# GpSimd instead of VectorE copies the low parts of the expert weights, in halves, four slots ahead

## The reference, cut to what matters

```
router_logits = xf @ router_w.T                 # 8192 tokens, 8 experts
topv, topi = top_k(softmax(router_logits), 2)   # two experts for each token
g = xf @ gate_w[e] + gate_b[e]                  # 128 -> 256
u = xf @ up_w[e] + up_b[e]                      # 128 -> 256
h = silu(g) * u
expert_out = h @ down_w[e] + down_b[e]          # 256 -> 128
y = sum over the token's two experts of probs * expert_out
```

## Time and profile before

| what | us |
|---|---|
| median of 3 executions without profiler | 1462.38 (1460.31 to 1465.81) |
| span of the profiled execution, first to last instruction | 1622.8 |
| what lies around the span | the profile gives no time of the profiled execution but its span |
| first expert stage in the profile (first row load to last scatter) | about 777 to 1041 |
| second expert stage in the profile | about 1314 to 1574 |

### The profile page before, as it was taken

The page is one execution under the profiler, slowest core; times in us unless marked ns, Lnnn a source line. Parts: engine busy times, 40 slices in busy tenths (PEclk is TensorE's granted clock), DMA queues, the critical chain, the costliest instruction groups (busy, mean ns, idle before and its releaser), DMA issues. The chain is left out here.

```text
span 1622.8 us, 37888 instructions
## 1 busy us (share of the span) xinstructions
PE 1206.8 (74%) x11717; PEld 1014.2 (62%) x11717; DVE 1149.5 (71%) x3828; ACT 943.0 (58%) x2002; POOL 980.7 (60%) x1152
## 2 busy tenths in 40 slices
PE   3779998888888888972688788476766357887850
PEld 1557777776777777752688787355555257877850
DVE  5379998888888888864555555388888645555538
ACT  2478888887888888841444444266666334444420
POOL 4245687777777777676255555438788735555540
PEclk9599999999999999996789898799899679998875
DMA  7121111111111111131222222112222132222228
GB/s 206 53 76 47 43 58 55 56 56 57 57 57 57 56 57 57 36 116 52 77 75 77 80 77 71 59 51 71 77 80 67 41 90 77 76 77 74 77 72 283
DMA packets 100819, 120.94 MB, mean 75 GB/s; under 512 B 17945, under 2 KB 80721, under 8 KB 100369
## 3 DMA queue, kind: packets, MB, share of 16 engines
q1 hardware_dynamic: 69600, 75.85, 15.9%
q0 software_dynamic: 17280, 35.95, 6.5%
q10 hardware_dynamic: 13744, 6.75, 1.5%
HBM read 49.45 MB, written 44.46 MB: 58 GB/s over the span
## 5 line engine op out<-in xcount | busy, mean ns | idle before, releaser
L1096 DVE TENSOR_TENSOR ebuf<-score_banks,region 128x768 f32<-128x768 f32 x256 | 243.8, 952 | 40.4 <-PE score_banks L809 34.8
L1337 ACT ACTIVATE region<-ebuf 128x768 f32<-128x768 f32 x256 | 215.4, 858 | 21.8 <-DVE ebuf L1096 21.8
L1315 ACT CAST copied<-max_banks 128x768 bf16<-128x768 f32 x256 | 205.4, 802 | 29.6 <-PE max_banks L797 27.3
L1755 POOL DMA_INDIRECT choice_rows<-first_yo,first_xg x142 | 136.7, 963 | 134.4 <-DVE first_yo L1875 100.0
L1755 POOL DMA_INDIRECT choice_rows<-second_yo,second_xg x142 | 137.3, 967 | 126.8 <-DVE second_yo L1875 92.4
L1625 POOL DMA_INDIRECT expert_rows<-d_rows,a_d_index x128 | 131.7, 1029 | 42.5 <-issue 30.8
L2171 POOL DMA_INDIRECT expert_rows<-d_rows,z_d_index x128 | 131.6, 1028 | 38.4 <-issue 32.1
L1831 ACT ACTIVATE first_silu<-first_bgu,first_biases 128x256 f32<-128x256 f32 x142 | 63.2, 478 | 131.6 <-PE first_bgu L1784 63.0
L1831 ACT ACTIVATE second_silu<-second_bgu,second_biases 128x256 f32<-128x256 f32 x142 | 63.1, 477 | 126.2 <-issue 61.3
L1514 POOL TENSOR_TENSOR rs<-arg,neghalf 128x4 f32<-128x4 f32 x32 | 37.1, 1161 | 137.8 <-DVE arg L1028 137.8
L1867 DVE SCALAR_TENSOR_TENSOR second_hT<-second_bgu,second_biases,second_silu 128x256 f32<-128x256 f32 x142 | 64.1, 478 | 74.9 <-ACT second_silu L1831 45.1
(11 more groups left out here) (333 smaller groups left out, 4386.0 us busy)
## 6 DMA issues: line engine op xcount, KB each, us to landing
region_r<-region_r SPq DMA_DIRECT2D x192, 128.0 KB
first_xg<-expert_rows SPq DMA_DIRECT2D x71, 132.0 KB
second_xg<-expert_rows SPq DMA_DIRECT2D x71, 132.0 KB
z_rows<-choice_rows SPq DMA_DIRECT2D x32, 256.0 KB
c_rows<-choice_rows SPq DMA_DIRECT2D x16, 512.0 KB
out<-xres ACTq DMA_DIRECT2D x16, 256.0 KB
choice_rows<-first_yo,first_xg POOLq DMA_INDIRECT x142
choice_rows<-second_yo,second_xg POOLq DMA_INDIRECT x142
```

Source lines behind the costliest of these rows:

```text
L1096: nc.vector.tensor_tensor(ebuf[:, half_of_ebuf(c, j), :, :], score_banks[:, :, 0:BK], bias32[:, plain(j), :], ALU.add).then_inc(scores_fre ...
L1315: nc.scalar.copy(copied[:, 2 * j:2 * j + 2, :], max_banks[:, :, 0:BK]).then_inc(maxed_free, 1)
L1337: nc.scalar.activation(p32[:, j % 4, :, :], ebuf[:, half_of_ebuf(c, j), :, :], ACT.Exp).then_inc(exped, 1)
L1755: pool.indirect_dma_start(choice_dram, bass.IndirectOffsetOnAxis(ap=xg[:, i % G, t, E:E + 1].bitcast(I32), axis=0), yo[:, i % 4, t, :], No ...
```

## The change

`wlo` gets four buffers in place of two. DVE no longer copies it. POOL copies it in two halves of 128x256 (gate, up). The halves of slot i + 4 stand behind the two scatters of slot i, one behind each; those of slots 0 to 3 stand ahead of the first scatter. POOL loads the packed word of experts for itself, once in four slots, and waits for `gu_full` of slot i before it overwrites that slot's buffer. PE waits for two increments of `wl_ready` for each slot in place of one. Nothing that is computed changes.

```diff
-        whi, wlo = sb("whi", [P, 2, 2 * EF], F32R), sb("wlo", [P, 2, 2 * EF], F32R)
+        whi, wlo = sb("whi", [P, 2, 2 * EF], F32R), sb("wlo", [P, 4, 2 * EF], F32R)
...
             @block.gpsimd
             def _(pool):
-
+                def lower_weights(i, e, parts):
+
+                    if i >= 4:
+                        pool.wait_ge(gu_full, i * NF + (NF - 4 * NF))
+                    for k in parts:
+                        at = slice(k * EF, (k + 1) * EF)
+                        nc.gpsimd.tensor_copy(wlo[:, i % 4, at], w["lo"][:, bass.ds(e, 1), at].rearrange("p a f -> p (a f)")
+                                              ).then_inc(wl_ready, 1)
+
+                def expert_from(i):
+                    k = i // 4
+                    word = pool.value_load(expert[0:1, k:k + 1], min_val=0, max_val=NE ** 8 - 1)
+                    return lambda j: (word >> (3 * (j - 4 * k))) & (NE - 1)
+
+                e = expert_from(0)
+                for i in range(4):
+                    lower_weights(i, e(i), range(2))
                 for i in range(ST):
+                    if i % 4 == 0 and i + 4 < ST:
+                        e = expert_from(i + 4)
                     pool.wait_ge(y_done, i + 1)
                     for t in range(2):
                         pool.indirect_dma_start(
                             choice_dram, bass.IndirectOffsetOnAxis(ap=xg[:, i % G, t, E:E + 1].bitcast(I32), axis=0),
                             yo[:, i % 4, t, :], None,
                         ).then_inc(stored[i % 4], 16)
+                        if i + 4 < ST:
+                            lower_weights(i + 4, e(i + 4), (t,))
...
-                    wh, wl = whi[:, i % 2, :], wlo[:, i % 2, :]
+                    wh, wl = whi[:, i % 2, :], wlo[:, i % 4, :]
                     pe.wait_ge(wh_ready, i + 1)
-                    pe.wait_ge(wl_ready, i + 1)
+                    pe.wait_ge(wl_ready, 2 * i + 2)
...
-
-                    if i >= 2:
-                        dve.wait_ge(gu_full, i * NF - 2)
-                    nc.vector.tensor_copy(wlo[:, i % 2, :], w["lo"][:, bass.ds(e, 1), :].rearrange("p a f -> p (a f)")).then_inc(wl_ready, 1)
```

## The result

The changed kernel takes 1537.21 us (median of 4 executions, 1533.02 to 1540.59); before it is 1462.48 (1460.31 to 1465.81; a fourth execution has come to the three whose median was 1462.38). The ratio is 1.0509, with a 95% interval of 1.0489 to 1.0529: 75 us, or 5.1%, slower. The forecast was 1540 us.

A forecast was written before the change was run, and what follows sets the result against it. PE at 2.54 us a slot was taken to bound the expert stages, POOL at 2.52 just under. With POOL at 3.12, (3.12 − 2.54) × 67 = 39 us a stage, 78 for two: 1462.4 + 78 = 1540 us, range 1485 to 1610.

The forecast's parts named there:

- The pace of the timed execution, 2.54 us a slot: Both expert stages, timed without a profiler, run without the profile's pauses: 2.54 us a slot, not 3.52.
- POOL's slot, 3.12 us: In the expert stages, two scatters, two copies and their gaps take POOL 3.12 us a slot in place of 2.52.
- The price of the copy from a small cast and the slope of memsets: A 128x256 POOL copy costs 0.40 us: 0.190 for a 128x4 cast plus 0.83 ns for each further element.
- rival D: The copies cost as the two-input row, or register work isn't covered as well: 1590 to 1630 us; chance 14%.
- Register work costs nothing: POOL's added register work runs during scatters and costs nothing; uncovered it would be 0.23 us a slot, 31 us in all.
- PE sets the pace before, POOL just under it: In unbroken stretches of the expert stages PE sets the pace at 2.54 us a slot, with POOL at 2.52.
- VectorE's relief is worth nothing: DVE loses a copy of 0.33 us a slot but isn't on the path, with 1.97 of 2.54 us: worth nothing.
- Rival B: With real pauses, each slot restarting after one is 0.33 us shorter without DVE's copy: 1441 us; chance 4%.
- rival C: Scatters get shorter without DVE's copy blocking POOL's memory port, up to 0.42 us a slot: 1484 us; chance 4%.
- Rival A: The expert stages' pauses are real, at 3.52 us a slot, and POOL's work fits in: 1460 to 1480 us; chance 10%.
- Rival E: PE idles 0.58 us in each slot and its clock stays at the lower level: above 1660 us; chance 3%.
- The lead of four slots and PE's wait: Copies for gate_up(i + 4) are 1 us early for a lone slot; within two slots that margin is gone and PE waits.

The follow-up runs named there:

- experiment 1: The kernel before with four buffers for the lower weights in place of two, VectorE still copying them: 1459.89 us, ratio 0.9998.
- Experiment 5: The kernel before without gate_up's product of upper weights and low x, four of twelve matmuls: 1460.57 us, ratio 0.9992.
- Experiment 4: The kernel before, where nobody copies lower weights from slot 2 on and PE uses those of slots 0 and 1: 1461.00 us, ratio 0.9998.
- experiment 6: The changed kernel without gate_up's product of upper weights and low x: 1532.45 us, ratio 1.0496.
- experiment 2: The kernel before, VectorE's copy kept, with POOL also making two copies a slot into a tile nobody reads: 1545.72 us, ratio 1.0579.
- experiments 3 and 7: The changed kernel with, in 3, only the first half on POOL, VectorE copying the other: 1498.18 us; in 7, one 128x512 POOL copy behind the second scatter: 1525.46 us.

## Why the prediction was right

1. **The pace of the timed execution, 2.54 us a slot.** This was the step on which it rested, and it held: 179.7 us from first to last scatter in experiment 1 is (179.7 − 1.26) / 70 = 2.55 us a slot. The argument was the difference between span and median. One sentence in it was wrong: that attention shows nothing. 26 us of the excess lay ahead of the first expert stage.
2. **POOL's slot, 3.12 us.** Measured 3.11. The copy is 0.408 for 0.40, the scatter 0.98 behind a copy for 0.958, the gap between them under 0.01 for 0.03, and 0.17 ahead of a scatter as forecast. None of the three is off by more than 0.03 us; that they cancel is luck.
3. **The price of the copy from a small cast and the slope of memsets.** The slope between 128x256 and 128x512 is 0.82 ns; the memsets gave 0.83. The other rate that the Trainium skill ("GPSIMD Engine Reference", section 3.1) has, 1.8 cycles an element, would by the prediction's estimate have made 0.57 us. With 0.408 measured it doesn't hold for this copy. The same number takes away the first half of rival D.
4. **Register work costs nothing.** Right: copies start within 0.01 us of the scatter's end. That is the other half of rival D.
5. **PE sets the pace before, POOL just under it.** The number was right and the order isn't shown. In experiment 1 PE (2.55 us a slot) and POOL (2.52) are both full. Experiment 5 shows that POOL is a bound of its own in the kernel before: with about 2.06 us of PE's work a slot the stage stays at 179.3 us. That PE would hold the stage at 2.54 us if POOL had less to do is argued from its lack of waits; no run takes work off POOL. For the sum it matters little: counted from 2.52 us the price is 0.02 × 134 = 3 us more. Either way, whatever was put on POOL had no cover from the start.
6. **VectorE's relief is worth nothing.** Experiment 4: ratio 0.9998. Rival B is out. So is rival C by the same run, which takes the copies off VectorE and gets nothing back from the scatters; in the changed kernel they even got longer, 980 ns for 958.
7. **Rival A** (real pauses) gave 1460 to 1480 us; 1537 was measured, and no other profile has the pauses.
8. **Rival E** (PE's clock): the granted clock is 0.99 in the changed kernel's stage, as in experiment 1's. Idle times of (219.00 − 190.53) / 71 = 0.4 us a slot did nothing to it, nor did those of experiment 6, (218.20 − 159.93) / 71 = 0.8 us.
9. **The lead of four slots and PE's wait.** Waiting for the lower weights sets in at slot 5, the second slot whose copies stand behind scatters, and so "within two slots" as forecast. The margin of 1 us was a little too large: it left out the time from down's end to the start of the addition that makes y, 0.57 us at the median in experiment 1. The sum doesn't use it. And the lead itself doesn't matter: experiment 2, in which PE waits for no weights of POOL, is no faster.
10. **What the profile would show.** The span was to grow by less than 78 us; it fell by 87, since the pauses weren't a property of the kernel. The wait of gate_up for POOL's copy is there in 66 of 71 slots, though the profile's own label says ACT.

## What to carry to other kernels

Before work is moved to an engine that looks half idle, ask for its pace in a stretch without pauses: in the profile before, POOL was busy 136 of 250 us, but there a slot's two scatters already took as long as PE's whole slot. When the span of the profiled execution is far above the median, the idle shares are those of the wrong execution; the unbroken stretches are the ones to count with. An engine that only stores results is on the path as soon as its slot is the longest, whether or not anyone waits for what it was given in addition, since the buffers that it frees are waited for. And before a wait is put down to the engine that the profile names, count which slot that engine's instruction belongs to.

## What was unexpected of the hardware

One profiled execution of the kernel before took 160 us more than its median, with pauses of some microseconds between a matmul's end and its reader: in each expert stage 19 of the 142 pieces of silu start over 1.5 us behind the end of the matmul that they read, the latest over 5 us behind. None of the profiles of the other kernels had a single one. A scatter behind a copy is 980 ns, and 958 behind another scatter (medians; the two kinds stand side by side in experiments 3 and 7). A POOL copy of 128x256 beside VectorE's 128x512 copies took up to 697 ns, against at most 433 in the changed kernel, which has none.
